# Causal attentions of a decoder: even score steps, shifts on GpSimd, banks in pairs for the exponentials, key tiles added on VectorE

## The reference

```python
q, k, v = split(x @ c_attn_w.T + c_attn_b)                  # 16 heads of 8
q_lat, k_lat = rope(q @ q2l_w.T + q2l_b), rope(k @ kv2l_w.T + kv2l_b)   # 32 wide
v_lat = v @ kv2l_w.T + kv2l_b
att = softmax(causal((q_lat @ wqk_w.T + wqk_b) @ k_lat.T * 32 ** -0.5))
y = (att @ v_lat) @ l2o_w.T + l2o_b                         # back to 8 per head
out = y.reshape(B, T, C) @ cproj_w.T + cproj_b
```

## Time and profile before

| what | value |
|---|---|
| median of 3 runs | 4223.95 us (4214.59 to 4225.65) |
| the profiled execution's own time | 4192.95 us |
| its span | 4191.1 us |
| TensorE, matmuls busy | 89% of the span |
| TensorE, weight loads busy | 57% |
| VectorE | 58% |
| ScalarE | 36% |
| GpSimd | 20% |
| DMA | 14 GB/s on the mean |
| granted TensorE clock, mean | 0.96 of full |

### The profile page before, as it was taken

How to read it: one execution, slowest core, us unless ns; L and a number is a source line. 1 busy time by engine, 2 the same in 40 slices (tenths; PEclk the granted TensorE clock), 3 DMA queues, 4 the chain that set the end, 5 groups by cost and what they waited for, 6 DMA issues and landing times. The chain is left out here.

```text
span 4191.1 us, 95747 instructions
## 1 busy us (share of the span) xinstructions
PE 3748.0 (89%) x38732; PEld 2389.5 (57%) x38732; DVE 2446.0 (58%) x6058; ACT 1525.1 (36%) x3430; POOL 829.2 (20%) x1464
## 2 busy tenths in 40 slices
PE   6998999988898889999979989999788988899999
PEld 3886885433354436665548868854333544366655
DVE  5767675565535466555466777656555344765554
ACT  4445443222222235532244454432222222354322
POOL 1441541010000104220024424400110001033200
PEclk9999999999999999999989999999989999999999
DMA  2000000100000000010010000001000000000100
GB/s 93 3 3 1 3 3 12 41 12 1 21 1 20 1 1 25 1 40 25 5 34 3 3 1 3 3 12 52 1 1 21 1 20 2 12 14 1 40 29 6
DMA packets 8680, 60.05 MB, mean 14 GB/s; under 512 B 893, under 2 KB 5297, under 8 KB 5937
## 3 DMA queue, kind: packets, MB, share of 16 engines
q1 hardware_dynamic: 8240, 53.90, 3.4%
HBM read 52.85 MB, written 1.05 MB: 13 GB/s over the span
## 5 line engine op out<-in xcount | busy, mean ns | idle before, releaser
L97 PE MATMUL psum<-ident_bf 128*128 128x512 bf16 x1528 | 399.3, 393 | 71.6 <-DVE l_attn_peak L930 54.7
L3106 ACT ACTIVATE l_attn_ax<-psum 128x128 f32<-128x128 f32 (+1 forms) x768 | 186.7, 279 | 394.2 <-PE psum L2921 274.8
L3345 DVE TENSOR_TENSOR l_attn_xx<-l_attn_xx,psum 128x256 f32<-128x256 f32 x512 | 205.3, 420 | 209.0 <-PE psum L2940 197.5
L438 ACT ACTIVATE l_ffn_silu<-psum 128x512 f32<-128x512 f32 (+2 forms) x208 | 124.2, 597 | 465.6 <-PE psum L404 411.2
L97 PEld LDWEIGHTS psum<-ident_bf 128*128 128x128 bf16 x1528 | 147.6, 102 | 250.0 <-DVE l_attn_peak L930 69.3
L503 DVE TENSOR_TENSOR l_ffn_hidden<-l_ffn_silu,psum 128x512 f32<-128x512 f32 (+2 forms) x176 | 120.5, 687 | 282.5 <-ACT l_ffn_silu L438 282.4
L103 PEld LDWEIGHTS psum<-streamed_weights,l_ffn_hidden 128*128 128x128 f32 (+2 forms) x1664 | 215.7, 192 | 121.2 <-issue 110.5
L2936 PE MATMUL psum<-l_attn_ax,l_attn_xx 64*64 64x64 f32 x5120 | 269.9, 225 | 0.0
L2940 PE MATMUL psum<-l_attn_xx,l_attn_ax 64*64 64x64 f32 x5120 | 261.9, 221 | 0.0
L3232 POOL TENSOR_TENSOR l_attn_part<-l_attn_ab,streamed_weights 128x128 f32<-128x128 f32 x640 | 245.8, 416 | 39.4 <-PE psum L2921 20.3
L930 DVE TENSOR_REDUCE l_attn_peak<-psum 128x4 f32<-128x2048 f32 (+3 forms) x128 | 186.5, 1488 | 99.4 <-PE psum L822 98.7
(11 more groups left out here) (535 smaller groups left out, 7843.4 us busy)
## 6 DMA issues: line engine op xcount, KB each, us to landing
streamed_weights<-pack_l_ffn SPq DMA_DIRECT2D x2, 5284.0 KB, 15.3
streamed_weights<-pack_l_attn SPq DMA_DIRECT2D x3, 2848.5 KB, 10.2
streamed_weights<-pack_l_ffn SPq DMA_DIRECT2D x2, 3972.0 KB, 12.7
streamed_weights<-pack_l_xattn SPq DMA_DIRECT2D x2, 2496.0 KB, 10.0
streamed_weights<-pack_l_ffn SPq DMA_DIRECT2D x2, 2192.0 KB, 8.3
streamed_weights<-pack_l_xattn SPq DMA_DIRECT2D x2, 2048.0 KB, 7.7
streamed_weights<-pack_l_ffn SPq DMA_DIRECT2D x2, 1923.0 KB, 7.9
streamed_weights<-pack_l_attn SPq DMA_DIRECT2D x2, 1107.5 KB, 5.2
```

What stands on the lines that cost most here:

```text
L97: pe.matmul(self.bank(bank), self.ident_bf[:, :], self.ident_bf[:, :].unsqueeze(1).to_broadcast([P, NT, P]), start=True, stop=True)
L3106: act.activation(ax[b, p, :, :], m.psum[b, p, 0:P].rearrange("p (i t) -> p i t", i=2), ACT.Copy).then_inc(ax_ready, 1)
L3345: dve.tensor_tensor(both, both, m.psum[:, p, P:384], ALU.subtract).then_inc(x_less, 1)
```

## The change

- The list of score steps holds scores alone, so lower and upper banks alternate strictly; the turns and the fillers of that phase go.
- GpSimd makes the shifts, and `coarse` and `shift` hold all four groups. Turns 0 and 1 come after the last step, turns 2 and 3 after the products of units 0 and 1, in banks 0 and 1.
- Banks 2 to 7 are three pairs that the exponentials go round; a unit takes two pairs, its exponential is two instructions, and TensorE starts on the next unit once the first of them is out.
- Values and sums of all groups add up in bank 0 and bank 1, in both layers. For groups 0 to 2 the sums of the first 128 columns are taken from key tile 0 directly; for the other 384 VectorE adds the key tiles into `total` (three additions per group), and `sums` multiplies that by ones. From unit 3 on an exponential waits for the addition that reads its slot (`totalled`). The last group's sums are all TensorE's.
- Layer 1 applies `l2o` to the values ahead of the attention instead of to its result: four latents, one product with `l2o`, a turn back, and four copies into a zeroed `v` on ScalarE; the additions with the bias go, and the rows of `cproj` are reordered to fit.
- The projection stands at the end of the same block, half by half; the second block goes.

Three copies lay between the maxima; now two stand ahead of the table load and one behind each of the next first halves. The core of the diff (removed lines that the new ones replace one for one stand in the kernel above):

```diff
-def causal_attention(m, name, q_of, k_of, head_of, v, ones_of, shared, mixed, early=None):
+def causal_attention(m, name, q_of, k_of, head_of, v, mixed, w_out):
...
-    steps = []
-    for g in range(G):
-        for i in reversed(range(NT)):
-            steps.append(("scores", g, i))
-            if g > 0 and i == 2:
-                steps.append(("turn", g - 1, 0))
+    steps = [(g, i) for g in range(G) for i in reversed(range(NT))]
     parts = [[(0, 0)], [(1, 0), (3, 3 * P)], [(2, 0)]]
     units = [(g, part) for g in range(G) for part in parts]
     diagonals = [sum(len(part) for _, part in units[0:u + 1]) for u in range(len(units))]
+    U = len(units)
+    HALF = T // 2
+    VALUES, SUMS, RING = 0, 1, 2
+    pair = lambda u, half: RING + 2 * ((2 * u + half) % 3)
...
+        total = sb("total", [P, 2, R, T - P])
...
-                def turn(g, bank):
+                def turn(g):
                     pe.wait_ge(shift_ready, g + 1)
+                    if g >= 2:
+                        pe.wait_ge(shiftT_ready, g - 1)
                     for t in range(NT):
...
                     ins.then_inc(shift_psum, 1)
...
                 def shifted(u):
                     g, part = units[u]
                     if u == 0:
-                        wait_consumed(pe, len(steps) - 2)
-                        m.warm(pe, 3, 5)
-                        wait_consumed(pe, len(steps) - 1)
+                        pe.wait_ge(peak_ready, NT * G)
                         pe.wait_ge(cleared, 2)
                     else:
-                        m.warm(pe, 6 if u == 1 else 0, 7)
-                        pe.wait_ge(exps_ready, u)
...
+                        pe.wait_ge(exps_ready, 2 * u - 1)
+                    for n, (j, c) in enumerate(part):
                         for r in range(R):
...
+                            pe.matmul(m.psum[:, pair(u, r // 2) + r % 2, c:c + T - j * P], k_of(g)[quad(r), j * P:(j + 1) * P],
                                       q_of(g)[quad(r), j * P:T], start=True, stop=False)
+                        if n == 0 and u % len(parts) == 0:
+                            pe.wait_ge(shiftT_ready, g + 1)
                         for r in range(R):
...
+                            ins = pe.matmul(m.psum[:, pair(u, r // 2) + r % 2, c:c + T - j * P], one_bf[W * r:W * r + 2, :],
                                             shiftT[W * r:W * r + 2, g, j * P:T], start=False, stop=True)
...
+                            if n == len(part) - 1 and r % 2 == 1:
+                                ins.then_inc(shifted_psum, 1)
                 def mix(u):
                     g, part = units[u]
                     pe.wait_ge(causal, diagonals[u])
                     if u == 0:
                         pe.wait_ge(shiftT_ready, G)
...
+                    if g == G - 1:
+                        for j, c in part:
                             for r in range(R):
...
+                                ins = pe.matmul(m.psum[quad(r), SUMS, j * P:T], m.const["ones_of"][:, g, :],
+                                                prob[:, u % SLOTS, r, c:c + T - j * P], start=False, stop=True,
+                                                skip_group_check=True)
...
+                    elif u % len(parts) == 0:
+                        for r in range(R):
+                            pe.matmul(m.psum[quad(r), SUMS, 0:P], m.const["ones_of"][:, g, :], prob[:, u % SLOTS, r, 0:P],
+                                      start=g == 0, stop=True, skip_group_check=True)
                     for j, c in part:
...
+                        for r in range(R):
+                            ins = pe.matmul(m.psum[quad(r), VALUES, j * P:T], v[:, j, head_of(g, r), :],
...
+                def sums(g):
+                    pe.wait_ge(totalled, 3 * g + 3)
+                    for r in range(R):
+                        ins = pe.matmul(m.psum[quad(r), SUMS, P:T], m.const["ones_of"][:, g, :], total[:, g % 2, r, :],
+                                        start=False, stop=True, skip_group_check=True)
+                    ins.then_inc(sums_psum, 1)
+                for n, (g, i) in enumerate(steps):
+                    base = 4 * (n % 2)
+                    if n >= 2:
+                        pe.wait_ge(peak_ready, n - 1)
+                    for r in range(R):
...
+                pe.wait_ge(peak_ready, NT * G - 1)
+                turn(0)
+                turn(1)
                 for u in range(U + 2):
                     if u < U:
                         shifted(u)
-                    if u == 0:
...
-                    if u >= 2:
+                    if u < 2:
+                        turn(2 + u)
+                    else:
+                        if u == U + 1:
+                            pe.wait_ge(exps_ready, 2 * U - 2)
+                            m.side.turn(pe, [m.psum[:, pair(U - 2, 1), t * P:(t + 1) * P] for t in range(NT)])
                         mix(u - 2)
...
+                        if u >= 2 + len(parts) and (u - 2) % len(parts) == 0:
+                            sums((u - 2) // len(parts) - 1)
+                m.warm(pe, 8, pair(U - 1, 0))
+                pe.wait_ge(exps_ready, 2 * U)
+                for half in range(2):
+                    pe.wait_ge(mixed_ready, half + 1)
+                    for t in (2 * half, 2 * half + 1):
+                        pe.matmul(m.psum[:, OUT, t * P:(t + 1) * P], mixed[:, 0, t * P:(t + 1) * P], w_out,
+                                  start=t == 0, stop=True, skip_group_check=True)
...
+                def copy(g):
+                    act.wait_ge(shift_psum, g + 1)
+                    act.activation(shiftT[:, g, :], m.bank(g % 2), ACT.Copy).then_inc(shiftT_ready, 1)
+                copy(0)
+                copy(1)
                 for u, (g, part) in enumerate(units):
...
                     if u >= SLOTS:
                         act.wait_ge(group_mixed, u - SLOTS + 1)
...
+                        if u - SLOTS < len(parts) * (G - 1):
+                            act.wait_ge(totalled, u - SLOTS + 1)
+                    for half in range(2):
+                        act.wait_ge(shifted_psum, 2 * u + half + 1)
+                        base = pair(u, half)
+                        act.activation(prob[:, u % SLOTS, 2 * half:2 * half + 2, 0:used(part)],
+                                       m.psum[:, base:base + 2, 0:used(part)], ACT.Exp).then_inc(exps_ready, 1)
+                        if half == u < 2:
+                            copy(2 + u)
...
+                pool.wait_ge(cleared, 2)
+                for g in range(G):
+                    pool.wait_ge(peak_ready, NT * (g + 1))
+                    pool.tensor_copy(coarse[:, g, :, :], peak[:, g, :, :]).then_inc(coarse_ready, 1)
+                    pool.wait_ge(coarse_ready, g + 1)
+                    pool.tensor_copy(shift[:, g, :, :, 0], coarse[:, g, :, :])
+                    pool.tensor_tensor(shift[:, g, :, :, 1], peak[:, g, :, :], coarse[:, g, :, :],
+                                       ALU.subtract).then_inc(shift_ready, 1)
                 for u, (g, part) in enumerate(units):
-                    pool.wait_ge(exps_ready, u + 1)
+                    pool.wait_ge(exps_ready, 2 * u + 2)
...
-                    if i == 0:
-                        dve.wait_ge(peak_ready, NT * (g + 1))
-                        if g >= 2:
-                            dve.wait_ge(shift_psum, g - 1)
-                        dve.tensor_copy(coarse[:, g % 2, :, :], peak[:, g, :, :]).then_inc(coarse_ready, 1)
-                        dve.wait_ge(coarse_ready, g + 1)
-                        if g == 0:
-                            dve.wait_ge(cleared, 1)
-                        dve.tensor_copy(shift[:, g % 2, :, :, 0], coarse[:, g % 2, :, :])
-                        dve.tensor_tensor(shift[:, g % 2, :, :, 1], peak[:, g, :, :], coarse[:, g % 2, :, :],
-                                          ALU.subtract).then_inc(shift_ready, 1)
...
+                for g in range(G - 1):
+                    first = len(parts) * g
+                    out = total[:, g % 2, :, :]
+                    dve.wait_ge(causal, diagonals[first + 1])
+                    if g >= 2:
+                        dve.wait_ge(sums_psum, g - 1)
+                    dve.tensor_tensor(out, prob[:, 0, :, P:T], prob[:, 1, :, 0:T - P], ALU.add).then_inc(totalled, 1)
+                    dve.wait_ge(totalled, first + 1)
+                    dve.tensor_tensor(out[:, :, 2 * P:3 * P], out[:, :, 2 * P:3 * P], prob[:, 1, :, 3 * P:T],
+                                      ALU.add).then_inc(totalled, 1)
+                    dve.wait_ge(causal, diagonals[first + 2])
+                    dve.wait_ge(totalled, first + 2)
+                    dve.tensor_tensor(out[:, :, P:3 * P], out[:, :, P:3 * P], prob[:, 2, :, 0:HALF],
+                                      ALU.add).then_inc(totalled, 1)
                 for half in range(2):
                     cols = slice(HALF * half, HALF * half + HALF)
...
```

(23 more changed lines are left out.)

180 lines of the change are left out of this document (54 added, 126 removed).

## The result

The changed kernel takes 4105.49 us (median of 4 runs, 4100.79 to 4111.57) against 4224.4 before; the ratio is 0.9724, with a 95% interval of 0.9709 to 0.9739. By the ratio that is 116.6 us (the medians lie 118.9 apart), where 89 were forecast. The forecast of 4135 was 30 us too high; the measured time lies inside its range.

The account below looks back on a forecast made before the run. Cycles of waits, not a full engine, bound score and exponential phases. Terms 46 - 11 + 35 - 1.4 + 14.6 + 6 = 89 us off gave 4135 us; the 8-in-10 range was 4065 to 4187.

Parts of the forecast that it names:

- Scores: First score matmul to last maximum: alternating steps without turns, shifts and fillers take 31.1 us a stage; gain 46 us, ends 30 and 77.
- two parts in three at 1.2 GHz: Weight given to TensorE's lower clock in the score phase, between 27.2 us (2.4 GHz) and 33.0 us (1.2 GHz), giving 31.1.
- as sparse, in every group: Score phase: without fillers, step 2 to the next step 3 holds two short steps in some 4.5 us, favouring the low clock.
- To the first exponential: Last maximum to first exponential: turns 0 and 1 now come first, 3.0 us instead of 1.6; loss 11 us, ends 5 and 17.
- Exponentials: Exponential phase: half-unit release, limited by additions and collisions, takes 32.2 us a stage; gain 35 us, ends 14 and 60.
- TensorE's room: Exponential phase: TensorE's work was put at 5.7 us a group at 2.4 GHz, under 8.
- The 0.8 for a start at the lower clock: Exponential phase: 0.8 us a stage added to 31.45 for TensorE starting at the lower clock, giving 32.2.
- Tail: Last exponential to last multiplication: last group's sums all on TensorE, 8.0 us a stage; loss 1.4 us in all.
- After the tail: Last multiplication to next stage: half the projection runs under the second half's reciprocal, one barrier goes; gain 14.6 us.
- Preparation: Ahead of layer 1's attention: VectorE's four additions into `v` go; 1.5 us a stage, gain 6 us, ends 0 and 10.
- Additions twice as dear: Rival, exponential phase: VectorE's additions take 3.5 us each, phase 37.5 us, total 4177 us; chance 0.08.
- the low clock through the exponentials: Rival: TensorE stays at 1.2 GHz, groups take 11.4 us, 62 us slower, 4286 us; chance 0.11 for the low clock throughout.

Follow-up runs that it names:

- eight profiles: Profiles of the change and of follow-up kernels that keep its score steps; score phases 225.2 to 235.7 us in sum, 231.2 on the mean.

## Why the prediction was right, and where its terms were off

- **Scores, 46 forecast and 68.9 measured.** The mechanism and the length of a group (6.65 us, 6.7 forecast) were right. The step that failed is "two parts in three at 1.2 GHz". By its own ends, 27.2 and 33.0, the 28.2 of the change is one part in six, and the mean of eight profiles, 28.9, three in ten. The granted clocks say much the same: 0.91 on the mean of these phases in the change is 18% of the time at 1.2 GHz, 0.85 in the eight profiles 31%. So "as sparse, in every group" was wrong. The sign "a granted clock there under 0.8" came in two stages of eight.
- **To the first exponential, -11 and -7.4.** I took 3.0 us for every stage; they were 1.86 to 3.38, the long ones by the clock at the turns or by the table load.
- **Exponentials, 35 and 53.1.** The groups were forecast at 7.9, 8.35, 9.45 and 5.75 and came at 7.73, 8.07, 8.54 and 5.64. The addition was sized right (1.76). The step that failed is the order on GpSimd in the third: I let bias and select both go first, but the addition got in behind the bias, and the select waited. With the wait for GpSimd the additions did read 2.16 and 2.64, over the 1.8 that I had called a sign of being wrong; the forecast held the same wait as a term of its own. TensorE's room was sized too well: 6.1 us busy a group instead of 5.7, and it, not VectorE, ended the gap at the first boundary. The 0.8 for a start at the lower clock did not come either: the clock was 1.00.
- **Tail, -1.4 and -6.2.** 8.60 us a stage, 8.0 forecast. I forgot the third group's sums, which TensorE does among the last products; without them, in the experiment with all sums on TensorE, the tail is 7.98.
- **After the tail, 14.6 and 13.6.** Right.
- **Preparation, 6 and -4.7.** In layer 1 the additions into `v` went, 2.48 us, but VectorE now waits nearly as much longer ahead of its rotations (in one place 2.0 us, whose releaser the profile does not show, in another 1.1 for TensorE), so sequence 0 gained 0.4. I had not seen that the next stage can start at the lower clock: 1.6 us in layer 1's stages of sequence 1 and 1.1 to 1.2 in layer 2's. With fillers in the idle stretches that did not occur.
- **Rivals.** Additions twice as dear did not come (1.76 us), nor the low clock through the exponentials (1.00). Both experiments that made TensorE idle more did bring part of that second rival: 0.84 to 0.87 in seven of eight stages with the turns back (0.98 in one), 0.80 to 0.93 with both halves awaited.

The errors of 23 and 18 us in the two large terms went the same way, the first by the clock, the second by GpSimd's order and, for 0.8 us a stage, by the clock; the tail and the preparation took 15.5 back. That the total came within 30 us is to this extent luck.

## What to carry to other kernels

In a cycle of waits between two engines, ask what takes a buffer without feeding the engine that runs dry: moving the turns out of the score steps gave 44 to 50 us over the eight stages, the engine that made the shifts nothing. Releasing a buffer in halves was worth more than the waits it saves by count, since, where it was undone, the clock fell as well. Sums put on VectorE gained under 5 us net, since they met GpSimd's selects on one side and lengthened the tail on the other; with a fourth slot, which takes the first of these out of the path, they gained 14.
